# First attention of a four-layer kernel: PSUM banks divided anew between scores and projections, and ScalarE's query copies moved ahead of the exponentials

## The chip, the cores and the metric

The kernel runs on one core of a Trainium2 chip. The metric is the device time of one launch in microseconds. The time before is the median of three runs, 1521.63 us (1520.63 to 1522.21).

## What is computed

Four layers, each an attention and a feed-forward part, over x of 8 x 128 tokens by 256 channels, with a context of the same shape. The change touches the first attention alone. Cut to what matters, it is:

```python
ln_out = _ln(hidden_states, ln_w, ln_b)
q = _ln(_fp8_linear_pertensor(ln_out, wq, wq_scale, q_in_scale).reshape(b, s, g, hpg, d), qln_w, qln_b)
k = _ln(_fp8_linear_pertensor(ln_out, wk, wk_scale, k_in_scale).reshape(b, s, g, d), kln_w, kln_b)
v = _fp8_linear_pertensor(ln_out, wv, wv_scale, v_in_scale).reshape(b, s, g, d)
core = _gqa(q, k, v).reshape(b, s, nh * d)
qx = _ln(_fp8_linear_pertensor(ln_out, wqx, wqx_scale, qx_in_scale).reshape(b, s, g, hpg, d), qxln_w, qxln_b)
kx, vx = jnp.split(jnp.einsum('bsi,oi->bso', cond, w_kv_x), 2, axis=-1)
xout = _gqa(qx, _ln(kx.reshape(b, sc, g, d), kxln_w, kxln_b), vx.reshape(b, sc, g, d)).reshape(b, s, nh * d)
cat = jnp.concatenate([core, xout], axis=-1)
return jnp.einsum('bsi,oi->bso', _div_clamp_fp8(cat, proj_smooth), wproj) * (proj_in_scale * proj_w_scale)
```

`_gqa` is softmax attention with 16 query heads of 128 over 8 key heads. There is a cross part (keys and values from the context) and a core part (from x itself).

## The kernel before

The first attention works on 16 tiles of 128 tokens: the eight tiles of x with the cross part, then the same eight with the core part. Each tile has eight units, one for each step: `UNITS` is k0, q0, k1, q1, v0, q2, v1, q3. A unit is one projection into a PSUM bank of 128 x 512: four heads of queries, of keys or of values. A query or key unit is normalised by head, transposed, and its scores, softmax, mix and output projection follow some steps later.

The order of the work is written by hand. `march` walks over global steps, and at each step every engine issues those functions whose due step it is, in the order of that engine's list. For a unit projected at step s: ScalarE squares it at s; VectorE sums the squares at s+1 (`variance`) and GpSimd makes the reciprocal root (`rstd`); VectorE normalises at s+2 (`normalise`), which reads the projection bank for the last time; TensorE transposes at s+3 (`turn`) and ScalarE copies that out at s+3 (`keep_turned`, L753 for queries, L758 for keys). Query units go on: `score` on TensorE and `row_max` on VectorE at s+4, `exponentials` on ScalarE and `row_inverse` on VectorE at s+5, `scale_probs` on ScalarE at s+6, `turn_probs` on TensorE and `keep_probs` on ScalarE at s+7, `mix` on TensorE and the first half of `round_mixed` on VectorE at s+8, the second half on GpSimd at s+9, `project_out` on TensorE at s+11. Value units are copied out by ScalarE at s+1 (`keep_values`), which frees their bank.

Queries are projected at odd steps, keys and values at even ones. So an even step on TensorE is `turn_probs`, `project_out`, `turn` of a query, and the projection of a key or value unit; an odd step is `score`, `mix`, sometimes `turn` of a key, and the projection of a query unit. Two steps make a period; four periods make a tile. On VectorE an even step is `variance` of a query, `row_inverse`, `normalise` of a key (steps 2 and 4 of a tile only), `add_to_x` (step 2), `quantise` of a part of the next tile's input (three parts a tile, at steps 4, 6 and 8, in the core part; one, at step 4, in the cross part up to its last tiles); an odd step is `variance` of a key (steps 1 and 3), `row_max`, `normalise` of a query, `round_mixed`.

Banks: three rotate over the projections (`bank_of`), one each holds the transposes, the scores, the transposed probabilities, the mix and the output projection. `project` waits until the unit three before it has been read out, `score` waits until the exponentials of the score before have been made (`exp_done`).

Some tiles carry work of their own on ScalarE and VectorE: splitting and centring weights (`prepare` in tile 0, the keys' and values' weights in tile 1, the queries' in tile 4 and at the end of the cross part). The last tile also starts the feed-forward part (`turn_first`, `first_up`) in banks that the attention has left.

Of the kernel before, what the change touches and what calls it, by code (L numbers as in the profile page):

```python
# [186 lines left out]
def layer0_attention(nc, top, res, w, before):  # L187
# [6 lines left out]
    PLAIN = [i for i, unit in enumerate(UNITS) if unit[0] == "v"]  # L194
    QUERY = [i for i, unit in enumerate(UNITS) if unit[0] == "q"]
    NN, NV, NA = len(NORMED), len(PLAIN), len(QUERY)
    BATCH = 4
# [3 lines left out]
    with phase_memory(nc, "l0a") as mem:  # L201
# [98 lines left out]

        proj_bank, turn_bank, score_bank = res.banks[0:3], res.banks[3], res.banks[4]
        probs_bank, mix_bank, out_bank = res.banks[5], res.banks[6], res.banks[7]

        def bank_of(b, i):
            return proj_bank[(b * STEPS + i) % 3]

        at_norm, at_plain, at_query = NORMED, PLAIN, QUERY

        def later(due, n):
            return [s + n for s in due]  # L310
# [5 lines left out]
        F_TURN = [12, 13]  # L316
        f_banks = (bank_of(F_TILE, NORMED[-2]), bank_of(F_TILE, PLAIN[-1]))
        F_UP = [QUERY[-1] + 8, QUERY[-1] + 10, QUERY[-1] + 11, QUERY[-1] + 12]

# [49 lines left out]
        def _(pe):  # L369
# [10 lines left out]
            def project(b, i):  # L380
                kind, u = UNITS[i]
                core = b >= TILES
                G = b * STEPS + i
                if G >= 3:
                    pb, pi = divmod(G - 3, STEPS)
                    if pi in NORMED:
                        norm_done.wait(pe, norm_done.at(pb, NORMED.index(pi) + 1))
                    else:
                        values_done.wait(pe, values_done.at(pb, PLAIN.index(pi) + 1))
# [31 lines left out]
            def score(b, a):  # L421
                turned_out.wait(pe, turned_out.at(b, NORMED.index(QUERY[a]) + 1))
                turned_out.wait(pe, turned_out.at(b, NORMED.index(UNITS.index(("k", a // 2))) + 1))
                exp_done.wait(pe, exp_done.at(b, a))
                for h in range(HU):
                    g = 2 * (a % 2) + h // 2
                    mm = pe.matmul(score_bank[:, h * P:(h + 1) * P], q_t[:, h * P:(h + 1) * P],  # L427
                                   k_t[:, a // 2, g * P:(g + 1) * P], start=True, stop=True)
                mm.then_inc(scored.sem, 1)
# [29 lines left out]
            def turn_first(k):  # L459
                pe.wait_ge(f_rows_ready, 2 * k + 2)  # L460
                if k == 0:
                    norm_done.wait(pe, norm_done.at(F_TILE, NN - 1))
                else:
                    values_done.wait(pe, values_done.at(F_TILE, NV))
                for i in range(2):
                    for c in range(KC):
                        at = (i * KC + c) * P
                        mm = pe.transpose(f_banks[k][:, at:at + P], f_rows[:, 2 * k + i, c * P:(c + 1) * P], res.ident[:])
                mm.then_inc(f_turned, 1)

            def first_up(k):
                if k == 0:
                    norm_done.wait(pe, norm_done.at(VTS - 1, NN))
                    values_done.wait(pe, values_done.at(VTS - 1, NV))
                    turned_out.wait(pe, turned_out.at(VTS - 1, NN))
                    pe.wait_ge(f_xn_ready, 2)
                    pe.wait_ge(res.loaded["l0_e_gate"], 16)
# [14 lines left out]
        def _(v):  # L492
# [115 lines left out]
            def row_max(b, a):  # L608
                scored.wait(v, scored.at(b, a + 1))
                v.tensor_reduce(neg_max[:, a, :], heads(score_bank), X, ALU.max, negate=True).then_inc(max_ready.sem, 1)  # L610

# [63 lines left out]
        def _(act):  # L675
# [70 lines left out]

            def keep_turned(b, n):
                core = b // TILES
                kind, u = UNITS[NORMED[n]]
                turned.wait(act, turned.at(b, n + 1))  # L750
                if kind == "q":
                    scored.wait(act, scored.at(b, u))
                    act.activation(q_t[:], turn_bank[:], ACT.Identity, scale=q_affine[:, core, 0:1],  # L753
                                   bias=q_affine[:, core, 1:2]).then_inc(turned_out.sem, 1)
                else:
                    scored.wait(act, scored.at(b - 1, 2 * u + 2))
                    name = "kln" if core else "kxln"
                    act.activation(k_t[:, u, :], turn_bank[:], ACT.Identity, scale=res.col(f"L0_xattn_{name}_w"),  # L758
                                   bias=res.col(f"L0_xattn_{name}_b")).then_inc(turned_out.sem, 1)

            def exponentials(b, a):
# [4 lines left out]
                for h in range(HU):  # L766
                    done = act.activation(probs[:, a % 2, h * P:(h + 1) * P], score_bank[:, h * P:(h + 1) * P],  # L767
                                          ACT.Exp, bias=neg_max[:, a, h:h + 1], accum_out=row_sum[:, a, h:h + 1])
# [34 lines left out]
            def keep_first(k):  # L803
# [5 lines left out]

            march(VTS, STEPS, [(exponentials, later(at_query, 5)), (scale_probs, later(at_query, 6)),  # L810

                               (keep_values, later(at_plain, 1)), (keep_turned, later(at_norm, 3)),
                               (prepare, range(STEPS)), (keep_probs, later(at_query, 7)), (square, at_norm),
# [2845 lines left out]
```

## Time and profile before

| what | value |
|---|---|
| median of three runs | 1521.63 us |
| the profiled execution's own time | 1520.4 us |
| its span | 1518.6 us |
| mean granted TensorE clock | 0.991 |
| the first attention in it | from about 20 to 470 us |
| PE busy over the span | 1432.2 us (94%) |
| VectorE, ScalarE, GpSimd busy | 887.6, 766.8, 528.6 us |

The engines are PE (TensorE's matmuls), PEld (its weight loads), DVE (VectorE), ACT (ScalarE) and POOL (GpSimd). PE's busy time is that of pipelined instructions whose ends are modelled, and a matmul's duration runs into the next one's. So in this case distances are read from start to start.

### The profile page before, as it was taken

Reading aid. Unit: us, or ns where it says so; the run is one execution under the profiler, and the core shown is the slowest. Engines: PE = TensorE matmul, PEld = TensorE weight load, DVE = VectorE, ACT = ScalarE, POOL = GpSimd, SP = SyncE. Lnnn points to the kernel's source line nnn. Section 1 sums busy time; section 2 is a strip of 40 time slices with the busy share of each in tenths; the row PEclk is TensorE's granted clock in tenths of the full one; section 3 lists DMA queues with packets and bytes.
Section 4 is the critical chain, followed back from the end, with each engine's and each line's share of the span. In section 5 each row is a group of like instructions: output and inputs, shape, how many; then the busy total and the mean of one; then the engine's idle time right before and its main releaser. Section 6 shows DMA issues by size and latency. Waiting matters only on the chain. (4 is left out here: it accounts for less than half of the span.)

```text
span 1518.6 us, 22221 instructions
## 1 busy us (share of the span) xinstructions
PE 1432.2 (94%) x6908; PEld 1030.3 (68%) x6910; DVE 887.6 (58%) x1934; ACT 766.8 (50%) x2122; POOL 528.6 (35%) x519
## 2 busy tenths in 40 slices
PE   3999999899999999999999999998997999999998
PEld 1677777787875555557878888866764666665656
DVE  7788888888875342323454545354677555553322
ACT  4888888888883211110234444444357555554210
POOL 2657577877762000000434243422111333321000
PEclk9999999999999999999999999999998999999999
DMA  5111000200005611112100000000232000011120
GB/s 201 65 58 60 8 5 2 95 1 1 2 1 201 234 51 53 52 49 90 66 1 1 1 1 1 14 15 4 103 148 95 1 1 1 1 29 38 49 67 19
DMA packets 21303, 71.65 MB, mean 47 GB/s; under 512 B 3858, under 2 KB 6290, under 8 KB 18244
## 3 DMA queue, kind: packets, MB, share of 16 engines
q1 hardware_dynamic: 12980, 57.37, 10.1%
q10 hardware_dynamic: 8208, 12.87, 2.7%
q8 instruction: 57, 0.93, 0.2%
q14 instruction: 58, 0.48, 0.1%
HBM read 69.01 MB, written 1.22 MB: 46 GB/s over the span
## 5 line engine op out<-in xcount | busy, mean ns | idle before, releaser
L1190 ACT ACTIVATE l0f_silu<-bank 128x512 f32<-128x512 f32 x48 | 28.6, 597 | 198.3 <-PE bank L1114 188.2
L828 POOL TENSOR_TENSOR l0a_stepped<-l0a_y,l0a_m 128x512 f32<-128x512 bf16 x64 | 74.1, 1158 | 94.4 <-DVE l0a_m L575 92.8
L856 POOL TENSOR_TENSOR l0a_head_rstd<-l0a_head_var,all_minus_half 128x4 f32<-128x4 f32 x96 | 101.8, 1064 | 8.4 <-DVE l0a_head_var L597 8.3
L1293 DVE TENSOR_TENSOR l0f_product<-l0f_silu,bank 128x512 f32<-128x512 f32 x48 | 32.9, 687 | 122.3 <-ACT l0f_silu L1190 122.2
L427 PEld LDWEIGHTS bank<-l0a_k_t,l0a_q_t 128*128 128x128 f32 x512 | 63.9, 193 | 50.1 <-ACT l0a_q_t L753 46.1
L767 ACT ACTIVATE l0a_work<-bank,l0a_neg_max 128x128 f32<-128x128 f32 x256 | 90.2, 370 | 1.2 <-DVE l0a_neg_max L610 1.2
L1722 DVE TENSOR_TENSOR all_weights_a<-bank,all_cols 128x512 f32<-128x512 f32 x64 | 43.9, 690 | 79.7 <-PE bank L1557 47.0
L1126 PEld LDWEIGHTS bank<-all_weights_a,l0f_hidden 128*128 128x128 f32 x384 | 72.9, 190 | 25.2 <-issue 16.7
L427 PE MATMUL bank<-l0a_k_t,l0a_q_t 128*128 128x128 f32 x512 | 72.9, 286 | 17.4 <-ACT l0a_q_t L753 17.1
L1126 PE MATMUL bank<-all_weights_a,l0f_hidden 128*128 128x256 f32 x384 | 88.9, 379 | 0.0
L2315 PE MATMUL bank<-l3a_f_xn_t,all_weights_b 128*128 128x512 f32 x192 | 86.2, 593 | 0.0
L800 ACT ACTIVATE l0a_work<-l0a_work,l0a_row_inv 128x128 f32<-128x128 f32 x256 | 83.1, 425 | 3.7 <-DVE l0a_row_inv L614 3.6
L832 POOL TENSOR_TENSOR l0a_cat<-l0a_stepped,l0a_m 128x512 fp32r<-128x512 f32 x64 | 77.3, 1208 | 10.2 <-issue 9.4
L2611 POOL TENSOR_TENSOR l3a_probs<-l3a_probs,l3a_row_inv 128x512 f32<-128x512 f32 x32 | 33.3, 1042 | 130.0 <-DVE l3a_row_inv L2414 130.0
L1905 ACT ACTIVATE l1a_work<-bank,l1a_exp_bias,l1a_q_scale 128x128 f32<-128x128 f32 x128 | 56.9, 454 | 41.6 <-DVE l1a_exp_bias L1788 41.6
L605 DVE TENSOR_TENSOR l0a_work<-bank,l0a_head_rstd 128x512 f32<-128x512 f32 x96 | 65.1, 678 | 15.6 <-POOL l0a_head_rstd L856 15.5
L739 ACT ACTIVATE l0a_squares<-bank 128x512 f32<-128x512 f32 x96 | 58.3, 608 | 24.7 <-PE bank L409 16.8
L455 PE MATMUL bank<-l0a_wp_high,l0a_cat 128*128 128x256 f32 x256 | 69.5, 304 | 0.1
L597 DVE TENSOR_REDUCE l0a_head_var<-l0a_squares 128x4 f32<-128x516 f32 x96 | 65.6, 683 | 6.2 <-ACT l0a_squares L739 5.0
L418 PE MATMUL bank<-all_ident,l0a_work 128*128 128x128 f32 x384 | 58.9, 276 | 9.7 <-DVE l0a_work L605 9.7
L444 PE MATMUL bank<-l0a_probs_t,l0a_values 128*128 128x256 f32 x256 | 66.0, 380 | 0.2 <-ACT l0a_probs_t L774 0.2
L455 PE MATMUL bank<-l0a_wp_low,l0a_cat 128*128 128x256 f32 x256 | 63.7, 281 | 0.0
(437 smaller groups left out, 3756.6 us busy)
## 6 DMA issues: line engine op xcount, KB each, us to landing
l0f_spread<-l0f_weights ACTq DMA_DIRECT2D x32, 192.0 KB, 2.8
all_weights_a<-in_l_w_q SPq DMA_DIRECT2D x2, 2048.0 KB, 14.2
l0f_spread<-l0f_weights ACTq DMA_DIRECT2D x32, 128.0 KB, 2.8
all_weights_b<-in_l_e_gate_up SPq DMA_DIRECT2D x1, 3200.0 KB, 10.1
all_weights_b<-in_l_e_gate SPq DMA_DIRECT2D x1, 3072.0 KB, 10.1
all_weights_a<-in_l_e_up SPq DMA_DIRECT2D x4, 768.0 KB, 7.1
all_weights_a<-in_l_e_down SPq DMA_DIRECT2D x1, 3072.0 KB, 15.4
l3a_spread<-l3f_weights SPq DMA_DIRECT2D x10, 256.0 KB, 3.4
```

The source lines that it names most:

```text
L427: mm = pe.matmul(score_bank[:, h * P:(h + 1) * P], q_t[:, h * P:(h + 1) * P], k_t[:, a // 2, g * P:(g + 1) * P], start=True, stop=True)
L444: mm = pe.matmul(mix_bank[:, half * 2 * P:(half + 1) * 2 * P], values[:, a // 2, g * P:(g + 1) * P], probs_t[:, half * 2 * P:(half + 1) * ...
L455: mm = pe.matmul(out_bank[:, 0:D], cat[:, a % 2, h * P:(h + 1) * P], part[:, a * HU + h, :], start=(a == 0 and h == 0 and n == 0), stop=(a ...
L597: v.tensor_reduce(head_var[:, m % 2, :], squares[:], X, ALU.add).then_inc(var_ready.sem, 1)
L605: v.tensor_tensor(heads(norm_rows[:, m % 2, :]), heads(bank_of(b, NORMED[n])), along(head_rstd[:, m % 2, :], P), ALU.mult).then_inc(norm_d ...
L767: done = act.activation(probs[:, a % 2, h * P:(h + 1) * P], score_bank[:, h * P:(h + 1) * P], ACT.Exp, bias=neg_max[:, a, h:h + 1], accum_ ...
L800: done = act.activation(pr, pr, ACT.Copy, scale=row_inv[:, a, h:h + 1])
L828: done = g.tensor_tensor(stepped[:, 0:n], value, step, ALU.add)
L832: return g.tensor_tensor(out, stepped[:, 0:n], step, ALU.subtract)
L856: g.tensor_tensor(head_rstd[:, m % 2, :], head_var[:, m % 2, :], res.minus_half[:, 0:HU], ALU.pow)\
L1126: mm = pe.matmul(down_banks[t // 2][:, (t % 2) * D:(t % 2 + 1) * D], hidden[:, n % 2, t * P:(t + 1) * P], w_down[:, j, :], start=(j == 0 a ...
L2315: mm = pe.matmul(bank[:], w_gate_up[:, c, i * (NCH - 1) * P + col:i * (NCH - 1) * P + col + P], f_xn_t[:, c, h * HALF:(h + 1) * HALF], sta ...
```

## The change

Two banks take the projections in turn, and two take the scores; the bank that was the third of the projections is now the first of the scores. `project` waits for the unit two before it, where it waited for the one three before it; `score` waits for the exponentials two before it. On ScalarE `keep_turned` is divided into `keep_queries` and `keep_keys`, and `keep_queries` stands first in the list, ahead of `exponentials`. The two banks of `turn_first` and the wait in front of `first_up` follow the new division.

```diff
+    KEY = [i for i, unit in enumerate(UNITS) if unit[0] == "k"]
...
-        proj_bank, turn_bank, score_bank = res.banks[0:3], res.banks[3], res.banks[4]
+        proj_bank, turn_bank, score_bank = res.banks[0:2], res.banks[3], (res.banks[2], res.banks[4])
...
-            return proj_bank[(b * STEPS + i) % 3]
+            return proj_bank[(b * STEPS + i) % 2]
...
-        f_banks = (bank_of(F_TILE, NORMED[-2]), bank_of(F_TILE, PLAIN[-1]))
+        f_banks = (bank_of(F_TILE, PLAIN[-1]), bank_of(F_TILE, NORMED[-1]))
...
-                if G >= 3:
-                    pb, pi = divmod(G - 3, STEPS)
+                if G >= 2:
+                    pb, pi = divmod(G - 2, STEPS)
...
-                exp_done.wait(pe, exp_done.at(b, a))
+                exp_done.wait(pe, exp_done.at(b, a - 1))
...
-                    mm = pe.matmul(score_bank[:, h * P:(h + 1) * P], q_t[:, h * P:(h + 1) * P],
+                    mm = pe.matmul(score_bank[a % 2][:, h * P:(h + 1) * P], q_t[:, h * P:(h + 1) * P],
...
+                    exp_done.wait(pe, exp_done.at(VTS - 1, NA - 1))
...
-            def keep_turned(b, n):
+            def keep_queries(b, a):
                 core = b // TILES
-                kind, u = UNITS[NORMED[n]]
...
+            def keep_keys(b, u):
+                turned.wait(act, turned.at(b, NORMED.index(KEY[u]) + 1))
...
-            march(VTS, STEPS, [(exponentials, later(at_query, 5)), (scale_probs, later(at_query, 6)),
-
-                               (keep_values, later(at_plain, 1)), (keep_turned, later(at_norm, 3)),
+            march(VTS, STEPS, [(keep_queries, later(at_query, 3)), (exponentials, later(at_query, 5)), (scale_probs, later(at_query, 6)),
+
+                               (keep_values, later(at_plain, 1)), (keep_keys, later(KEY, 3)),
```

Most lines of the changed kernel in the stage stand one or two below their old numbers. On ScalarE, in an even step of the cross part and the odd step behind it (`l0a_q_t` is the queries' copy, `l0a_work` the exponentials and then the scaling, `l0a_probs_t` the copy of the transposed probabilities), before:

```order
L767 ACTIVATE l0a_work,l0a_row_sum<-bank4,l0a_neg_max 128x128 x4
L753 ACTIVATE l0a_q_t<-bank3,l0a_q_affine 128x512
L774 ACTIVATE l0a_probs_t<-bank5 128x512
L739 ACTIVATE l0a_squares<-bank1 128x4x128
L800 ACTIVATE l0a_work<-l0a_work,l0a_row_inv 128x128 x4
L758 ACTIVATE l0a_k_t<-bank3,all_cols 128x512
```

and now:

```order
L753 ACTIVATE l0a_q_t<-bank3,l0a_q_affine 128x512
L769 ACTIVATE l0a_work,l0a_row_sum<-bank2,l0a_neg_max 128x128 x4
L776 ACTIVATE l0a_probs_t<-bank5 128x512
L741 ACTIVATE l0a_squares<-bank0 128x4x128
L802 ACTIVATE l0a_work<-l0a_work,l0a_row_inv 128x128 x4
L760 ACTIVATE l0a_k_t<-bank3,all_cols 128x512
```

The copy of the queries, which waits for the transposes at the end of TensorE's even step, has moved in front of the four exponentials; nothing else has moved.

On TensorE the instructions stand as they did; what has changed is the banks, and with them what the waits are for. From a value unit's projection to the next query's, in the core part, before:

```order
L409 MATMUL bank2<-l0a_wv_high,l0a_xq 128x512 [waits l0a_w_low,l0a_quant_done,l0a_norm_done]
L409 MATMUL bank2<-l0a_wv_low,l0a_xq 128x512
L427 MATMUL bank4<-l0a_k_t,l0a_q_t 128x128 [waits l0a_exp_done,l0a_turned_out]
L427 MATMUL bank4<-l0a_k_t,l0a_q_t 128x128 x3
L444 MATMUL bank6<-l0a_probs_t,l0a_values 128x256 [waits l0a_mixed_read,l0a_values_done,l0a_probs_t_ready]
L418 MATMUL bank3<-all_ident,l0a_work 128x128 [waits l0a_turned_out,l0a_norm_done]
L409 MATMUL bank0<-l0a_wq_high,l0a_xq 128x512 [waits l0a_w_low,l0a_quant_done,l0a_norm_done]
```

and now:

```order
L410 MATMUL bank0<-l0a_wv_high,l0a_xq 128x512 [waits l0a_w_low,l0a_quant_done,l0a_norm_done]
L410 MATMUL bank0<-l0a_wv_low,l0a_xq 128x512
L428 MATMUL bank2<-l0a_k_t,l0a_q_t 128x128 [waits l0a_exp_done,l0a_turned_out]
L428 MATMUL bank2<-l0a_k_t,l0a_q_t 128x128 x3
L445 MATMUL bank6<-l0a_probs_t,l0a_values 128x256 [waits l0a_mixed_read,l0a_values_done,l0a_probs_t_ready]
L419 MATMUL bank3<-all_ident,l0a_work 128x128 [waits l0a_turned_out,l0a_norm_done]
L410 MATMUL bank1<-l0a_wq_high,l0a_xq 128x512 [waits l0a_w_low,l0a_quant_done,l0a_norm_done]
```

Keys and values now always use bank 0 and queries always bank 1, so the value unit here waits for the normalisation of the key unit two steps before it, and the query for that of the query before it.

On VectorE the order is the same; in an even step with a key's normalisation and the odd step behind it, it now reads:

```order
L616 RECIPROCAL l0a_row_inv<-l0a_row_sum 128x4 [waits l0a_exp_done]
L607 TENSOR_TENSOR l0a_work<-bank0,l0a_head_rstd 128x512 [waits l0a_turned,l0a_rstd_ready]
L571 TENSOR_SCALAR l0a_yq16<-l0a_yq16 128x256 [waits l0a_quant_scaled]
L573 TENSOR_SCALAR l0a_e16<-l0a_yq16 128x256
L577 TENSOR_SCALAR l0a_mq16<-l0a_e16 128x256
L612 TENSOR_REDUCE l0a_neg_max<-bank2 128x4 [waits l0a_scored]
L607 TENSOR_TENSOR l0a_work<-bank1,l0a_head_rstd 128x512 [waits l0a_turned,l0a_rstd_ready]
```

Bank 0 is read out for the last time by the second row and bank 1 by the last; each stands behind a row that waits for another engine.

## Rows read from the trace of the kernel before

**Rows 1.** The page, busy time by engine, and one of its groups of instructions.
```profile
PE 1432.2 (94%) x6908; PEld 1030.3 (68%) x6910; DVE 887.6 (58%) x1934; ACT 766.8 (50%) x2122; POOL 528.6 (35%) x519
...
L597 DVE TENSOR_REDUCE l0a_head_var<-l0a_squares 128x4 f32<-128x516 f32 x96 | 65.6, 683 | 6.2 <-ACT l0a_squares L739 5.0
```
**Rows 2.** Stretches of cross and core: length, busy PE, PEld, DVE, ACT, POOL, clock, DMA.
```profile
140.00:180.00 40.00, 39.34 (x234) 30.99 (x233) 35.05 (x72) 33.28 (x107) 25.98 (x26) 1.00 0.02 5
340.00:380.00 40.00, 37.07 (x237) 31.39 (x236) 34.32 (x76) 35.42 (x117) 31.26 (x33) 1.00 0.01 1
```
**Rows 3.** PE's waits over the span: us in total, times, longest.
```profile
PE bank L427 <- ACT l0a_q_t L753: 17.1, 30, 1.3
```
**Rows 4.** Timeline of one period of the core part: start, duration, engine, instruction.
```profile
352.17 0.35 ACT L767 ACTIVATE l0a_work<-bank,l0a_neg_max 128x128 f32<-128x128 f32 x1
...
352.28 0.60 PE L418 MATMUL bank<-all_ident,l0a_work 128*128 128x128 f32 x4
...
352.64 0.48 PE L409 MATMUL bank<-l0a_wk_high,l0a_xq 128*128 128x512 f32 x1
...
353.54 0.79 ACT L753 ACTIVATE l0a_q_t<-bank,l0a_q_affine 128x512 f32<-128x512 f32 x1
353.69 0.18 DVE L614 RECIPROCAL l0a_row_inv<-l0a_row_sum 128x4 f32<-128x4 f32 x1 [0.18 <-ACT l0a_work L767]
353.79 0.67 DVE L605 TENSOR_TENSOR l0a_work<-bank,l0a_head_rstd 128x512 f32<-128x512 f32 x1
354.20 0.62 ACT L774 ACTIVATE l0a_probs_t<-bank 128x512 f32<-128x512 f32 x1
...
354.38 1.16 PE L427 MATMUL bank<-l0a_k_t,l0a_q_t 128*128 128x128 f32 x8 [0.58 <-ACT l0a_q_t L753]
...
354.68 0.63 ACT L739 ACTIVATE l0a_squares<-bank 128x512 f32<-128x512 f32 x1
...
355.38 1.03 PE L444 MATMUL bank<-l0a_probs_t,l0a_values 128*128 128x256 f32 x4
...
356.24 0.60 PE L418 MATMUL bank<-all_ident,l0a_work 128*128 128x128 f32 x4
356.38 0.68 DVE L610 TENSOR_REDUCE l0a_neg_max<-bank 128x4 f32<-128x512 f32 x1
...
356.60 0.48 PE L409 MATMUL bank<-l0a_wq_high,l0a_xq 128*128 128x512 f32 x1
...
356.97 0.68 DVE L605 TENSOR_TENSOR l0a_work<-bank,l0a_head_rstd 128x512 f32<-128x512 f32 x1
...
359.00 0.60 PE L418 MATMUL bank<-all_ident,l0a_work 128*128 128x128 f32 x4
```
**Rows 5.** Timeline, the first and the last operation of one `quantise` on VectorE.
```profile
361.29 0.83 DVE L569 TENSOR_SCALAR l0a_yq<-l0a_yq 128x256 bf16<-128x256 bf16 x1
...
362.49 0.23 DVE L575 TENSOR_SCALAR l0a_mq<-l0a_e 128x256 bf16<-128x256 bf16 x1
```
**Rows 6.** Timeline: one cross projection, and VectorE's `add_to_x`, once a tile.
```profile
106.13 1.88 PE L399 MATMUL bank<-l0a_wkx,l0a_ctx_t 128*128 128x512 f32 x4
...
88.17 0.47 DVE L627 SCALAR_TENSOR_TENSOR all_x<-bank,l0a_out_scale,all_x 128x256 f32<-128x256 f32 x1
...
220.77 0.48 DVE L627 SCALAR_TENSOR_TENSOR all_x<-bank,l0a_out_scale,all_x 128x256 f32<-128x256 f32 x1
...
304.15 0.47 DVE L627 SCALAR_TENSOR_TENSOR all_x<-bank,l0a_out_scale,all_x 128x256 f32<-128x256 f32 x1
...
431.63 0.47 DVE L627 SCALAR_TENSOR_TENSOR all_x<-bank,l0a_out_scale,all_x 128x256 f32<-128x256 f32 x1
```
**Rows 7.** Start of the stage: one stretch of a microsecond (columns of Rows 2), then PE's timeline.
```profile
38.00:39.00 1.00, 0.61 (x3) 0.61 (x4) 1.00 (x2) 0.71 (x2) 1.00 (x2) 0.50 0.00 0
...
38.39 1.12 PE L418 MATMUL bank<-all_ident,l0a_work 128*128 128x128 f32 x4 [3.29 <-DVE l0a_work L605]
...
42.71 1.71 PE L427 MATMUL bank<-l0a_k_t,l0a_q_t 128*128 128x128 f32 x8
44.26 0.60 PE L418 MATMUL bank<-all_ident,l0a_work 128*128 128x128 f32 x4
```

More of the change, by code:

```diff
@@ L461, in turn_first @@
                 if k == 0:
-                    norm_done.wait(pe, norm_done.at(F_TILE, NN - 1))
+                    values_done.wait(pe, values_done.at(F_TILE, NV))
                 else:
-                    values_done.wait(pe, values_done.at(F_TILE, NV))
+                    norm_done.wait(pe, norm_done.at(F_TILE, NN))
                 for i in range(2):
@@ L609, in row_max @@
                 scored.wait(v, scored.at(b, a + 1))
-                v.tensor_reduce(neg_max[:, a, :], heads(score_bank), X, ALU.max, negate=True).then_inc(max_ready.sem, 1)
+                v.tensor_reduce(neg_max[:, a, :], heads(score_bank[a % 2]), X, ALU.max, negate=True).then_inc(max_ready.sem, 1)
             def row_inverse(b, a):
@@ L745, in keep_values @@
                 act.activation(values[:, n, :], bank_of(b, PLAIN[n])[:], ACT.Copy).then_inc(values_done.sem, 1)
-            def keep_turned(b, n):
+            def keep_queries(b, a):
                 core = b // TILES
-                kind, u = UNITS[NORMED[n]]
[L750 to L759, printed above, removed]
+                turned.wait(act, turned.at(b, NORMED.index(QUERY[a]) + 1))
+                scored.wait(act, scored.at(b, a))
+                act.activation(q_t[:], turn_bank[:], ACT.Identity, scale=q_affine[:, core, 0:1],
+                               bias=q_affine[:, core, 1:2]).then_inc(turned_out.sem, 1)
+            def keep_keys(b, u):
+                turned.wait(act, turned.at(b, NORMED.index(KEY[u]) + 1))
+                scored.wait(act, scored.at(b - 1, 2 * u + 2))
+                name = "kln" if b >= TILES else "kxln"
+                act.activation(k_t[:, u, :], turn_bank[:], ACT.Identity, scale=res.col(f"L0_xattn_{name}_w"),
+                               bias=res.col(f"L0_xattn_{name}_b")).then_inc(turned_out.sem, 1)
             def exponentials(b, a):
@@ L766, in exponentials @@
                 for h in range(HU):
-                    done = act.activation(probs[:, a % 2, h * P:(h + 1) * P], score_bank[:, h * P:(h + 1) * P],
+                    done = act.activation(probs[:, a % 2, h * P:(h + 1) * P], score_bank[a % 2][:, h * P:(h + 1) * P],
                                           ACT.Exp, bias=neg_max[:, a, h:h + 1], accum_out=row_sum[:, a, h:h + 1])
```

## The prediction

> **What bounds the kernel now.** I read the page's busy times first. TensorE is busy for 94% of the span [rows 1], so the reader should look for what TensorE waits for, and for what a change could put in front of it. The stretches by stage come next. In the cross part TensorE is busy for 39.34 us of 40, in the core part for 37.07; ScalarE and VectorE are at 83 to 89% in both [rows 2]. All three engines are near full, so slack on any of them is small. The list of waits then names what the change aims at: scores that wait for the copied queries, 17.1 us in 30 waits [rows 3]. Last, the timeline of one period shows why [rows 4]. ScalarE starts its exponentials at 352.17, before TensorE has begun to turn the next queries (352.28), and copies them only behind the exponentials, at 353.54. The score starts at 354.38, 0.58 us late.
>
> The same rows show what the early exponentials serve. They release VectorE's reciprocal (353.69), behind which stands the normalisation of a key unit (353.79). That frees a projection bank, and with three banks nobody needs it soon: the next key or value projection in that bank is a whole unit away.
>
> **The clock of one period.** Let 0 be the start of the turning of queries (352.28). From start to start [rows 4]: turn to projection 0.36; the transposes end at 0.60. A projection of four matmuls gives way to the next work after about 1.0 (estimate: the 2.40 from 356.60 to 359.00 hold one, with the turned probabilities and the output projection). Score to mix 1.00, mix to the key's turn 0.86, that to the query projection 0.36, and from there to the next turn 2.40. On ScalarE the copy of queries takes 0.66 to the next instruction, and a score may start 0.84 after the copy's start; the four exponentials take 1.37. On VectorE the reciprocal starts 1.52 after the first exponential, the normalisation 0.10 later; it lasts 0.67, and I give TensorE 0.05 to see it, as it needed after the copy. `row_max` to the next start is 0.59.
>
> **What is removed.** The score no longer waits for the exponentials, and the copy of queries no longer stands behind them. At most the 17.1 us of [rows 3] can be won. The exp_done wait itself was never last: the wait that ended last is the copy. So the second score bank is worth nothing beyond letting the copy go first.
>
> **What is added, keys and values.** Key unit 1 now waits for the normalisation of key unit 0, and value unit 0 for that of key unit 1: both belong to the same even step. The chain is closed: turn ends 0.60, the copy starts 0.64, the exponentials 1.30, the reciprocal 2.82, the normalisation 2.92, done at 3.59, and the projection starts at 3.64, where it started at 0.36. Behind it on TensorE stand the score, the mix and everything else; nothing covers the 3.04 us. This holds in two periods of four (call them A). The other two (B) wait for value unit copies of the step before, which are long done.
>
> **What is added, queries.** A query projection now waits for the normalisation of the query before, which stands behind `row_max` of the score of the same step. The least distance from score to query projection is then 1.16 + 0.05 + 0.59 + 0.67 + 0.05, about 2.5. TensorE has 1.86 of other work for that time, or 2.22 with a key's turn.
>
> **The mix.** It needs the copied probabilities, which stand behind copy and exponentials on ScalarE: 2.67 + 0.62 + 0.05 = 3.34 at the earliest.
>
> **The sum by period, core part** (measured: 127.5 us for five tiles, 25.5 a tile [rows 6]).
> - A at step 4: projection 3.64, score 4.64, its end 5.80, `row_max` 5.85, normalisation 6.44, query projection 7.16, next turn 9.56.
> - A at step 2: the key's variance comes in between. Its projection ends near 4.8, its square takes 0.6, the variance 0.68 [rows 1, 4]: 0.3 more, 9.86.
> - B at step 6: score 1.48, mix 3.34 to 4.20. VectorE: reciprocal 2.82, `quantise` 1.43 [rows 5] to 4.35, `row_max`, normalisation 4.94, query projection 5.66, next turn 8.06.
> - B at step 0: a variance more, 8.7.
> Together 36.2, 10.7 more a tile; eight tiles, 86 us.
>
> **Cross part** (132.6 us for five tiles, 26.5 a tile [rows 6]). A projection from the context lasts 1.88 against 1.16, 0.72 more [rows 4, 6]: A gives 10.3 and 10.6. B has no `quantise`: at step 6 the score starts 2.1, ends 3.3, and the next turn is at 7.0; at step 0 it is 8.2, since square and variance of the key come first. Together 36.1, 9.6 more; eight tiles, 77 us.
>
> **Tiles with weight work.** Centring and splitting stand on VectorE between its reciprocal and its `row_max`, so what was slack now delays query projections; the first and the last tile, on the other hand, have fewer full periods. I put the two at +7 together, with bounds of -15 and +40.
>
> So 86 + 77 + 7 = 170 us at full clock.
>
> **The clock.** At the start of the stage TensorE stood still for 3.29 us waiting for a normalisation; work went on at 38.39 with a granted clock of 0.50, and a score took 1.71 instead of 1.16; at 44.26 a turn is back at 0.60 [rows 4, 7]. 0.50 is the lower level, 1.2 GHz of 2.4. The new gap in A is 3.04 us, near to that row. The lower bound is nothing; the upper is 5.9 us at half speed, 3 us lost for each of the 32 gaps, 94 us. I take 1.6 each, since part of the work in it is overtaken by VectorE's chain and not each gap need drop the clock: 50 us.
>
> The Trainium skill ("TensorE: Matmul & The Clock Gate", HAM oscillation) describes a loop in which TensorE waits each round and its clock falls each round. By that rule all 32 gaps would pay, and the sum would be 264 and not 220. The row at 38.39 agrees with it for one gap; no row shows a repeated one.
>
> The skill ("Perfetto Trace Analysis", Matmuls) also asks that independent groups rotate through different banks so that reading one out overlaps the next one's matmuls. By that rule alone two and two is as good a rotation as three and one and the 17 us would be won; the timeline weighs against it, as a projection's read-out ends two steps later [rows 4].
>
> **Nothing** I count for: the wait in front of `first_up` (the last exponentials come steps earlier), the other banks of `turn_first` (their last readers are two or more steps old), SP and GpSimd (nothing moves there; they wait along).
>
> **Sum.** 1520.4 of the profiled execution + 170 + 50 = 1740; the median stands 1.2 above it: 1742.
>
> **Rivals.**
> 1. The clock stays high through gaps of 3.04 us. For: 3.29 is longer, and ScalarE's chain may be a little shorter than I have it. Against: it fell there. 1692. Chance 0.22.
> 2. Only the keys' wait and the mix bind, the query chain on VectorE is hidden. A then takes 9.3 and B 6.6 in the core part, 10.0 and 6.6 in the cross part: 32 and 33 a tile, +6.3 and +6.7, about 104, so 1626. Against: `row_max` cannot start before the score. Chance 0.08.
> 3. The clock also falls in B's gaps (0.7 and 1.5 us close together) and stays down longer: 3 us an A, 1.5 a B, 9 a tile, 144: 1836. Chance 0.15.
> 4. Faster: the projection banks are free in time. That would need a key's normalisation done within 0.36 of the turn's start, so VectorE would have to run it before the reciprocal that waits for the exponentials. Then the 17.1 us go: 1504. The order on VectorE speaks against it. Chance 0.02.
> 5. Gain and new waits cancel to within 0.2%: 0.01.
> The forecast has 0.52.
>
> 0.2% (3 us) is about what a measurement can tell from no change. Faster 0.02, same 0.01, slower 0.97. The range: between rivals 2 and 3, with the bounds of weight work, 1635 to 1850.
>
> **What would show it.** In the profile after: TensorE waiting for VectorE's normalisation at the projection line, about 3 us each, 32 times, about 90 to 100 us, and again 0.3 to 1.5 us before each query projection; the wait for the copied queries gone; ScalarE idle before the copy; a turn-to-turn distance near 9.7, 9.7, 8, 8.5; tiles 36 us apart at full clock; granted clock below 1 in the stage. The argument is wrong if key and value projections start within a microsecond of the turn, or if tiles stay below 30 us.

## The result and the profile after

The changed kernel takes 1745.36 us (median of four runs, 1742.6 to 1750.92) against 1521.13 us. The ratio is 1.148, with a 95% interval of 1.146 to 1.150. The forecast was 1742, its range 1635 to 1850. The profiled execution took 1743.94 us, of which 1742.2 are the span. From the page of the changed kernel, the busy times by engine and the clock in 40 slices:

```profile
PE 1518.2 (87%) x6910; PEld 1085.4 (62%) x6910; DVE 862.8 (50%) x1934; ACT 775.7 (45%) x2122; POOL 520.6 (30%) x519
...
PEclk9988978889988889999999999999989999999999
```

TensorE goes from 94% of the span [rows 1] to 87%, and the clock shows eights and a seven in ten of the slices 3 to 15 (87 to 653 us), the attention's. (TensorE's busy time has grown by 86 us although its work is the same: part of that is the slower clock.) The other engines' busy times moved by no more than 3%, over a longer span.

Where the time went is told first by the marks of `add_to_x`, one for each tile, as in [rows 6]. Timeline of the changed kernel, VectorE:

```profile
108.72 0.48 DVE L629 SCALAR_TENSOR_TENSOR all_x<-bank,l0a_out_scale,all_x 128x256 f32<-128x256 f32 x1
...
329.79 0.47 DVE L629 SCALAR_TENSOR_TENSOR all_x<-bank,l0a_out_scale,all_x 128x256 f32<-128x256 f32 x1
...
447.11 0.47 DVE L629 SCALAR_TENSOR_TENSOR all_x<-bank,l0a_out_scale,all_x 128x256 f32<-128x256 f32 x1
...
641.14 0.48 DVE L629 SCALAR_TENSOR_TENSOR all_x<-bank,l0a_out_scale,all_x 128x256 f32<-128x256 f32 x1
...
692.94 0.48 DVE L629 SCALAR_TENSOR_TENSOR all_x<-bank,l0a_out_scale,all_x 128x256 f32<-128x256 f32 x1 [4.82 <-PE bank L456]
```

Five cross tiles take 221.1 us (108.72 to 329.79), 44.2 each, where it was 26.5. Five core tiles take 194.0, 38.8 each, where it was 25.5. The last mark stands at 692.94 and stood at 470.69: 222.3 us later. The span grew by 223.6, so the loss lies in the first attention, but for about 1 us.

The list of TensorE's waits over the span then says what it waits for:

```profile
PE bank L410 <- DVE l0a_work L607: 101.2, 53, 3.6
PE bank L400 <- DVE l0a_work L607: 50.3, 16, 5.1
PE bank L445 <- ACT l0a_probs_t L776: 13.5, 19, 0.7
...
PE bank L428 <- ACT l0a_q_t L753: 1.7, 2, 0.9
```

L410 and L400 are the projections (L400 those from the context). They wait 151.5 us for VectorE's normalisations; in the kernel before no such wait stands in the list. The mix waits 13.5 us for the copied probabilities. The score's wait for the copied queries, 17.1 us in [rows 3], has fallen to 1.7. So the change took away the wait that it aimed at, and put about ten times as much waiting in its place.

One period, to be laid beside [rows 4]; a period of the core part in the changed kernel, TensorE, then ScalarE, then VectorE:

```profile
480.42 0.60 PE L419 MATMUL bank<-all_ident,l0a_work 128*128 128x128 f32 x4
484.09 0.79 PE L410 MATMUL bank<-l0a_wk_high,l0a_xq 128*128 128x512 f32 x1 [3.07 <-DVE l0a_work L607]
...
485.96 1.91 PE L428 MATMUL bank<-l0a_k_t,l0a_q_t 128*128 128x128 f32 x8
...
490.05 0.49 PE L410 MATMUL bank<-l0a_wq_high,l0a_xq 128*128 128x512 f32 x1
...
492.47 0.60 PE L419 MATMUL bank<-all_ident,l0a_work 128*128 128x128 f32 x4
...
481.05 0.78 ACT L753 ACTIVATE l0a_q_t<-bank,l0a_q_affine 128x512 f32<-128x512 f32 x1 [1.29 <-PE bank L419]
481.73 0.36 ACT L769 ACTIVATE l0a_work<-bank,l0a_neg_max 128x128 f32<-128x128 f32 x1
...
483.26 0.18 DVE L616 RECIPROCAL l0a_row_inv<-l0a_row_sum 128x4 f32<-128x4 f32 x1 [3.36 <-ACT l0a_work L769]
483.36 0.68 DVE L607 TENSOR_TENSOR l0a_work<-bank,l0a_head_rstd 128x512 f32<-128x512 f32 x1
```

With the turn of the queries at 480.42 as 0, the copy starts at 0.63, the exponentials at 1.31, the reciprocal at 2.84, the key's normalisation at 2.94 and the key projection at 3.67. The forecast chain had 0.64, 1.30, 2.82, 2.92 and 3.64. VectorE waited 3.36 us for the exponentials and TensorE 3.07 us for VectorE: neither was busy, and each was held by the instruction at the head of its own queue. The whole period takes 12.05 us, the slow clock behind the gap included.

The clock, in two stretches of the core part, one behind such a gap and one without (columns as in Rows 2):

```profile
484.00:490.00 6.00, 5.91 (x19) 5.06 (x20) 3.41 (x8) 1.76 (x5) 1.01 (x1) 0.50 0.00 1
...
503.00:511.00 8.00, 6.55 (x42) 5.21 (x41) 4.58 (x12) 5.59 (x18) 5.01 (x6) 1.00 0.01 3
```

Behind the gap TensorE worked for six microseconds at half its clock: the score at 485.96 lasts 1.91, against 1.16 in [rows 4]. In the period from 503.33, whose two waits are 0.7 us each (the mix at 506.69, the query projection at 508.54), the clock stays at 1.00.

### The profile page after: what moved, and what is told of

It reads as the page before. It is cut to its first block and busy times, and to the rows that moved or that the text cites. A ratio compares the mean times of both kernels' runs of the same rounds, so it can differ in the third digit from the quotient of the medians.

```text
span 1742.2 us, 22223 instructions
## 1 busy us (share of the span) xinstructions
PE 1518.2 (87%) x6910; PEld 1085.4 (62%) x6910; DVE 862.8 (50%) x1934; ACT 775.7 (45%) x2122; POOL 520.6 (30%) x519
## 5 line engine op out<-in xcount | busy, mean ns | idle before, releaser
L858 POOL TENSOR_TENSOR l0a_head_rstd<-l0a_head_var,all_minus_half 128x4 f32<-128x4 f32 x96 | 97.3, 1014 | 96.5 <-DVE l0a_head_var L599 96.4
L410 PE MATMUL bank<-l0a_wq_high,l0a_xq 128*128 128x512 f32 x128 | 61.2, 478 | 53.8 <-DVE l0a_work L607 52.0
L428 PEld LDWEIGHTS bank<-l0a_k_t,l0a_q_t 128*128 128x128 f32 x512 | 82.9, 234 | 30.4 <-issue 19.5
L616 DVE RECIPROCAL l0a_row_inv<-l0a_row_sum 128x4 f32<-128x4 f32 x64 | 11.4, 178 | 176.0 <-ACT l0a_work L769 176.0
L445 PE MATMUL bank<-l0a_probs_t,l0a_values 128*128 128x256 f32 x256 | 79.6, 440 | 14.8 <-ACT l0a_probs_t L776 13.5
L428 PE MATMUL bank<-l0a_k_t,l0a_q_t 128*128 128x128 f32 x512 | 85.4, 321 | 1.7 <-ACT l0a_q_t L753 1.7
L753 ACT ACTIVATE l0a_q_t<-bank,l0a_q_affine 128x512 f32<-128x512 f32 x64 | 49.8, 777 | 62.7 <-PE bank L419 62.7
L456 PE MATMUL bank<-l0a_wp_high,l0a_cat 128*128 128x256 f32 x256 | 75.4, 324 | 0.0
L410 PEld LDWEIGHTS bank<-l0a_wq_high,l0a_xq 128*128 128x128 f32 x128 | 26.0, 203 | 74.8 <-DVE l0a_work L607 68.5
```

Source lines behind the costliest of these rows:

```text
L410: mm = pe.matmul(bank[:], xq[:, b % 2, WHICH[kind], c, :], part[:, c, u * BANK:(u + 1) * BANK], start=(c == 0 and n == 0), stop=(c == KC - ...
L428: mm = pe.matmul(score_bank[a % 2][:, h * P:(h + 1) * P], q_t[:, h * P:(h + 1) * P], k_t[:, a // 2, g * P:(g + 1) * P], start=True, stop=True)
L445: mm = pe.matmul(mix_bank[:, half * 2 * P:(half + 1) * 2 * P], values[:, a // 2, g * P:(g + 1) * P], probs_t[:, half * 2 * P:(half + 1) * ...
L456: mm = pe.matmul(out_bank[:, 0:D], cat[:, a % 2, h * P:(h + 1) * P], part[:, a * HU + h, :], start=(a == 0 and h == 0 and n == 0), stop=(a ...
L858: g.tensor_tensor(head_rstd[:, m % 2, :], head_var[:, m % 2, :], res.minus_half[:, 0:HU], ALU.pow)\
```

## The experiments

Twelve kernels were run. The kernel before, run beside them, took 1520.42 to 1520.84 us; against that the change costs 225 us. Below, 0.63 or 3.67 "of the period" count from the start of the queries' turn. Diffs are against the changed kernel where nothing else is said; `...` stands for lines left out. The two parts of the change come first.

### The order on ScalarE alone

```diff
-        proj_bank, turn_bank, score_bank = res.banks[0:2], res.banks[3], (res.banks[2], res.banks[4])
+        proj_bank, turn_bank, score_bank = res.banks[0:3], res.banks[3], (res.banks[4], res.banks[4])
...
-            return proj_bank[(b * STEPS + i) % 2]
+            return proj_bank[(b * STEPS + i) % 3]
...
-                if G >= 2:
-                    pb, pi = divmod(G - 2, STEPS)
+                if G >= 3:
+                    pb, pi = divmod(G - 3, STEPS)
...
-                exp_done.wait(pe, exp_done.at(b, a - 1))
+                exp_done.wait(pe, exp_done.at(b, a))
```

> The changed order on ScalarE alone: three projection banks and one score bank as before, the copy of queries ahead of the exponentials. My theory (most of the loss is the third projection bank, the order adds to it): the score now waits for exponentials that start at 1.30 of the period and so starts at 2.83, the mix at 3.83, the next turn at 7.45 or 7.1, against 25.5 to 26.5 a tile 29.1: 50 us slower than before, 1571 (1545 to 1600). Rival, the order is the whole cause and the banks cost nothing: about 1745. Rival, the order costs nothing by itself: 1521.

Measured: 1570.26 us (1568.37 to 1571.1), ratio 1.0326 (1.0311 to 1.0341), 50 us slower than before. Its waits:

```profile
PE bank L428 <- ACT l0a_work L769: 68.9, 62, 2.4
```

That is the score waiting for the exponentials, which now stand behind the copy, 62 times in 64 scores. Five core tiles take 29.3 us each; 29.1 was worked out. The order costs 50 us where there is one score bank, and the mean clock is 0.990 (0.991 before).

### The banks alone

```diff
-            march(VTS, STEPS, [(keep_queries, later(at_query, 3)), (exponentials, later(at_query, 5)), (scale_probs, later(at_query, 6)),
+            march(VTS, STEPS, [(exponentials, later(at_query, 5)), (scale_probs, later(at_query, 6)),
...
-                               (keep_values, later(at_plain, 1)), (keep_keys, later(KEY, 3)),
+                               (keep_values, later(at_plain, 1)), (keep_queries, later(at_query, 3)), (keep_keys, later(KEY, 3)),
```

> The banks alone: two for projections and two for scores as in the changed kernel, ScalarE in its old order. My theory: the key's normalisation is done at 2.2 of the period and not at 3.6, so key and value projections start at 2.2; periods 8.2, 8.5, 7.0, 7.3 in the core part, 0.7 more in two of four in the cross part: 31 and 32.4 a tile, about 95 us more than before plus some 15 for the clock, 1630 (1600 to 1670). PE's wait at key and value projections about 1.5 us each. Rival, order alone is the cause: 1521. Rival, banks alone are the cause: 1745.

Measured: 1608.52 us (1608.21 to 1612.65), ratio 1.0588 (1.0568 to 1.0607), 88 us slower than before; 21 less than worked out, but inside what the theory gave, and far from both rivals. The mean clock is 0.988, so the 15 us that I had put in for it did not come. Its waits:

```profile
PE bank L410 <- DVE l0a_work L607: 63.0, 63, 2.6
PE bank L400 <- DVE l0a_work L607: 29.4, 16, 5.1
```

The 16 waits at L400, cross projections of keys and values, are 1.8 us on average, against 3.1 in the changed kernel. So 50 and 88 make 138, and the change as a whole costs 225: 87 more. The order puts the exponentials behind the turn, and the banks put the projection behind the exponentials. Only together do they close a chain from one TensorE instruction to the next one in its queue.

The chain by itself is the smaller part of these 87, as far as the core part shows it. In the changed kernel three periods in a row run at full clock; they take 9.91, 9.57 and 7.62 us:

```profile
443.57:470.67 27.10, 19.02 (x118) 15.62 (x117) 14.97 (x37) 17.77 (x54) 13.51 (x15) 1.00 0.00 1
```

The fourth takes 8.23 at full clock (from 551.70), so a tile is 35.3, or 9.8 more than before. A core tile costs 3.8 more with the order alone and 5.0 more with the banks alone (30.5), 8.9 together, both at a clock of 1.00 there. So the chain adds about 1 us a tile to the two. The other 3.5, up to the measured 38.8, are the clock, which neither part brings down there.

### The third bank back

The kernel has eight PSUM banks (`res.banks`), and three for projections, two for scores and one for each of the four other uses are nine. The mix can go into that score bank which is idle in its step:

```diff
-        proj_bank, turn_bank, score_bank = res.banks[0:2], res.banks[3], (res.banks[2], res.banks[4])
-        probs_bank, mix_bank, out_bank = res.banks[5], res.banks[6], res.banks[7]
+        proj_bank, turn_bank, score_bank = res.banks[0:3], res.banks[3], (res.banks[4], res.banks[6])
+        probs_bank, out_bank = res.banks[5], res.banks[7]
+
+        def mix_bank(a):
+            return score_bank[(a + 1) % 2]
...
+                mixed_read.wait(pe, mixed_read.at(b, a - 2))
...
+                exp_done.wait(pe, min(exp_done.at(b, a + 2), VTS * NA))
```

> The changed kernel with its third projection bank back. The room comes from the mix, which is written into that one of the two score banks that is idle in its step. Theory: with the read-out of three units back is free, all waits at the projection lines go, the clock is back at 1.00 in the stage, and what stays is the mix that waits for the copied probabilities until 3.34: periods 7.0 and 6.6, 27.1 a tile, 1540 (1525 to 1560). Rival, that the order on ScalarE is the cause: still over 1700.

Measured: 1548.54 us (1548.39 to 1549.06), ratio 1.0186 (1.017 to 1.0201), mean clock 0.991. With the third bank back, 197 of the 225 us are gone. The wait at the projections is gone from the list, and what stays is the mix:

```profile
PE bank L450 <- ACT l0a_probs_t L781: 25.8, 38, 0.7
```

28 us remain, nine more than expected; the core tile is at 27.5, where 27.1 was worked out, and the cross tile at 28.4.

### Two score banks with the old order

The same kernel with the two lines of ScalarE's list as in "The banks alone".

> Three projection banks, two score banks (shared with the mix as in the run with the third bank back) and ScalarE's old order. It is the control for the shared banks, and it asks whether a second score bank gives anything by itself. Theory: the score waits for the copied queries, not for the exponentials, so nothing is gained and nothing lost: 1521, within 3 us, with the waits of rows 3 unchanged near 17 us. Rival, a second score bank is worth what the waits show: 1504.

Measured: 1520.25 us (1518.25 to 1523.24), ratio 1.0000 (0.9991 to 1.0010). The score's wait is the old one, 16.3 us in 27 waits. So sharing the mix's bank costs nothing, and a second score bank by itself gives nothing: the wait for the exponentials was never the last one.

### Who reads the bank last, and where it stands in its queue

The next two keep the changed kernel's banks and move VectorE's instructions. First the keys' normalisation alone, ahead of the reciprocal (`normalise_keys` and `normalise_queries` are `normalise` for the one kind and the other):

```diff
-            march(VTS, STEPS, [(variance, later(at_norm, 1)), (row_inverse, later(at_query, 5)),
-                               (row_max, later(at_query, 4)), (normalise, later(at_norm, 2)),
+            march(VTS, STEPS, [(variance, later(at_norm, 1)), (normalise_keys, later(KEY, 2)), (row_inverse, later(at_query, 5)),
+                               (row_max, later(at_query, 4)), (normalise_queries, later(at_query, 2)),
```

> The changed kernel with the keys' normalisation alone moved ahead of row_inverse; the queries' stays behind row_max. It parts the two new waits. Theory: the 3 us waits before key and value projections go, those before query projections stay at 0.5 to 2 us each; periods about 7.6, 8.5, 7.7, 8.2 in the core part, and 1 to 2 us less in the cross part, clock nearly full: 1625 (1590 to 1660). Rival, the queries' wait is hidden behind the mix: 1545. Rival, the wait only moves over to the queries: over 1700.

Measured: 1642.49 us (1641.61 to 1643.84), ratio 1.0803 (1.0788 to 1.0818), inside what the theory gave: 103 us of 225 are gone. The mean clock is 0.980 and was 0.945, so a part of the 103 is the clock. Then all normalisations first:

```diff
-            march(VTS, STEPS, [(variance, later(at_norm, 1)), (row_inverse, later(at_query, 5)),
-                               (row_max, later(at_query, 4)), (normalise, later(at_norm, 2)),
+            march(VTS, STEPS, [(normalise, later(at_norm, 2)), (variance, later(at_norm, 1)), (row_inverse, later(at_query, 5)),
+                               (row_max, later(at_query, 4)),
```

> The changed kernel with VectorE's normalisations first in its list, ahead of variance, row_inverse and row_max. Theory: what hurts with two banks is that the last reader of a bank stands behind instructions that wait for this step's exponentials and score. With it first, waits at the projection lines fall from 151.5 us to under 30, the mix at 3.34 stays: 27 a tile, 1545 (1525 to 1580). Rival, two banks are too few wherever the reader stands: over 1650.

Measured: 1589.67 us (1586.92 to 1593.15), ratio 1.0456 (1.044 to 1.0472), mean clock 0.983: 53 more. The waits at the projections, with the keys first and with all first:

```profile
PE bank L410 <- DVE l0a_work L607: 76.0, 75, 3.6
...
PE bank L400 <- DVE l0a_work L607: 9.8, 14, 4.2
```

```profile
PE bank L410 <- DVE l0a_work L607: 34.9, 36, 2.7
...
PE bank L400 <- DVE l0a_work L607: 10.6, 14, 3.6
```

From 151.5 us the waits fall to 85.8 and then to 45.5. I had forecast under 30 and 1545: the mechanism is borne out, the remainder mis-sized. At 1590 two banks are still 41 us behind the kernel with three and the same order on ScalarE (1548.54). Three banks with the normalisations first were not run, so what moving them costs or gives by itself stays open. In one place of this run VectorE's own queue is in the way: at 382.47 a key's normalisation starts as soon as the last step of `round_mixed` is through, and the value projection follows at 383.21, 0.49 us late.

### How much of it is the clock

```diff
+            def idle_work(b, a):
+                if a > 1:
+                    return
+                mixed_read.wait(pe, mixed_read.at(b, a + 1))
+                for n in range(22):
+                    pe.matmul(mix_bank[:, 0:P], res.ident[:], res.ident[:], start=True, stop=True)
...
-                               (turn, later(at_norm, 3)), (project, range(STEPS))])
+                               (turn, later(at_norm, 3)), (idle_work, later(at_query, 9)), (project, range(STEPS))])
```

> The changed kernel with 22 extra matmuls (identity by identity, 128 columns, into the idle mix bank; nothing reads them) in each of the 32 places where TensorE waits for a key's normalisation. It sizes the clock's share. Theory: the waits stay as long, since the matmuls end before the wait does, but the granted clock in the stage goes from 0.87 to above 0.95, and the time falls by 40 to 70 us to 1690 (1675 to 1710). Rival, the clock costs nothing because VectorE's chain hides the slow matmuls: 1745 or a little above.

Measured: 1751.57 us (1749.03 to 1753.38), ratio 1.1518 (1.150 to 1.1535), far from the 1690 expected, and it looks like the rival. But the timeline shows that the added work did not fit into the gap:

```profile
493.44 5.08 PE L465 MATMUL bank<-all_ident 128*128 128x128 f32 x44
498.27 0.48 PE L410 MATMUL bank<-l0a_wv_high,l0a_xq 128*128 128x512 f32 x1
```

The 22 calls became 44 instructions, and the projection came 5.3 us behind the turn at 493.00 and not 3.67. So it was run again with `range(12)`.

> The changed kernel with 12 extra matmuls in each of the 32 gaps and not 22. In the run with 22 each call became two instructions, 44 of them took 5.08 us, and the projection started 5.3 us behind the turn where the wait alone ends at 3.67: 1.6 us too long, 32 times 51 us. If the clock's share is near 45 us the two cancel, as that run's 1752 has it, and 12 calls (2.8 us, inside the gap) give 1700 (1690 to 1712) with the same clock of about 0.97. If the clock costs nothing: 1745. If the 22 had cost nothing by their length: 1752.

Measured: 1702.44 us (1701.98 to 1705.98), ratio 1.1200 (1.1185 to 1.1216). More work in TensorE's queue makes the kernel 43 us faster. Here the added matmuls end inside the gap; of the wait 0.39 us is left, and it still ends with the normalisation:

```profile
489.30 0.60 PE L419 MATMUL bank<-all_ident,l0a_work 128*128 128x128 f32 x4
489.73 2.84 PE L465 MATMUL bank<-all_ident 128*128 128x128 f32 x24
492.97 0.50 PE L410 MATMUL bank<-l0a_wk_high,l0a_xq 128*128 128x512 f32 x1 [0.39 <-DVE l0a_work L614]
...
499.20 0.60 PE L419 MATMUL bank<-all_ident,l0a_work 128*128 128x128 f32 x4
```

The projection stands at 3.67 of the period, as in the changed kernel, and the period is 9.90 where that of the changed kernel was 12.05. The stretch from 60 to 660 us of the changed kernel, then of this one:

```profile
60.00:660.00 600.00, 448.94 (x2213) 349.32 (x2214) 307.53 (x683) 341.94 (x1033) 271.68 (x273) 0.87 0.04 15
```

```profile
60.00:660.00 600.00, 520.37 (x3159) 425.50 (x3158) 324.71 (x727) 364.11 (x1103) 289.57 (x288) 0.96 0.05 17
```

The granted clock goes from 0.87 to 0.96, and 43 us with it, as was expected (1700). As 0.96 is not 1.00, 43 is a lower bound of the clock's share. At most 182 of the 225 us are the waits and what stands behind them. In two of the five core tiles of this run the clock is 1.00, and they take 35.3 us, as the changed kernel's own periods gave it:

```profile
420.65:455.95 35.30, 30.55 (x200) 25.93 (x200) 19.79 (x50) 23.23 (x72) 19.15 (x20) 1.00 0.01 1
```

### Looking for a faster kernel

With three projection banks and two score banks, the copy of queries can stand between the second and third of the four exponentials. ScalarE then fills the time before the turn's end with two of them. Against the kernel with the third bank back (`exp_head` and `exp_tail` are the first and the last two exponentials):

```diff
-            march(VTS, STEPS, [(keep_queries, later(at_query, 3)), (exponentials, later(at_query, 5)), (scale_probs, later(at_query, 6)),
+            march(VTS, STEPS, [(exp_head, later(at_query, 5)), (keep_queries, later(at_query, 3)), (exp_tail, later(at_query, 5)), (scale_probs, later(at_query, 6)),
```

> Three projection banks, two score banks shared with the mix, and the copy of queries between the second and the third of the four exponentials, so that ScalarE fills the time before the turn's end with two of them. Theory: the copy starts at 0.64 of the period, the score at 1.48 where it was 2.10, the mix at 2.7 where it was 3.10: up to 0.4 us a period in the core part, less in the cross part, where TensorE is full: 1510 (1503 to 1519), faster than before. Rival, ScalarE is the bound and nothing is won: 1521. Rival, the later reciprocal takes it back: over 1525.

Measured: 1520.83 us (1519.3 to 1523.65), ratio 1.0007 (0.9998 to 1.0016): no difference, where 1510 was expected. The score's wait is gone, 1.7 us in 2 waits from 60 to 460 us where it was 16.5 in 28. In the same stretch the turns wait more:

```profile
PE bank L422 <- DVE l0a_work L612: 8.6, 16, 1.6
```

Before, it was 3.8 us in 8. Four core tiles pass in 25.05 us each and not 25.3, and that is lost again elsewhere (cross tiles 26.6 and not 26.5). TensorE's named waits are some 9 us fewer and the time is the same, so they come back in places that the list does not name; where, was not followed through. One case is seen in the timeline: the projection at 346.98 starts 0.82 behind its turn and not 0.36, just after GpSimd has written the input that it reads. So it isn't shown what bounds this kernel.

```profile
346.21 0.67 POOL L846 TENSOR_TENSOR l0a_xq<-l0a_stepped,l0a_mq 128x256 fp32r<-128x256 f32 x1
```

Since the normalisations in turn waited for GpSimd's reciprocal root, I put the root ahead of GpSimd's rounding passes: in this kernel, in the one with all normalisations first, and in the kernel before. The edit is the same in all three:

```diff
-            march(VTS, STEPS, [(round_mixed, later(at_query, 9)), in_tile(F_ROWS_TILE, first_rstd, F_ROWS[0:1]), (rstd, later(at_norm, 1)),
+            march(VTS, STEPS, [(rstd, later(at_norm, 1)), (round_mixed, later(at_query, 9)), in_tile(F_ROWS_TILE, first_rstd, F_ROWS[0:1]),
```

> The kernel with the copy between the exponentials, and GpSimd's reciprocal root ahead of its two rounding passes in an even step. In the run without it the score's wait was gone, but turns waited for the normalisation (15.9 us in 19 waits), which waited for the reciprocal root on GpSimd (10.2 us in the core part). Theory: with the root first these waits go and the gain shows, 1510 (1503 to 1517). Rival, TensorE's own work is the bound by now: 1520. Rival, the rounding comes too late for the output projection: over 1525.

> The changed kernel with normalisations first on VectorE (1590) and the reciprocal root first on GpSimd as well. Theory: of the 45.5 us that TensorE still waited at the projection lines, most is the root that stands behind the rounding passes; with it first 1560 (1548 to 1575), the rest being the mix that waits and the normalisation behind `round_mixed`. Rival, it is VectorE's own queue alone: 1590.

> The kernel before with the reciprocal root first on GpSimd and nothing else: the control for the run with the copy between. Theory: there TensorE waits for the copied queries and not for normalisations (2.7 us in the core part), so 1518 to 1521. Rival, the root alone brings what that run brings: 1510.

Measured, in this order: 1544.21 us (1542.49 to 1545.04), ratio 1.0153 (1.0139 to 1.0167); 1614.14 us (1613.24 to 1614.42), ratio 1.0613 (1.0597 to 1.063); 1530.67 us (1528.38 to 1531.97), ratio 1.0065 (1.0053 to 1.0078). All three expectations failed, and in each case the edit costs: 23, 24 and 10 us. For the first, the rival that the rounding comes too late has the right size and the right wait. From its waits, from 60 to 460 us, TensorE, then GpSimd:

```profile
PE bank L461 <- POOL l0a_cat L846: 18.6, 31, 1.5
```

```profile
POOL l0a_head_rstd L870 <- DVE l0a_head_var L604: 93.4, 53, 4.4
```

The root waits 93.4 us for VectorE's variance (1.6 without the edit) and holds up the rounding behind it, and the output projection, whose wait was in no list before, waits 18.6 us. In the third it waits 11.3. It is the fault of the change once more, on another engine: an instruction whose input comes late, moved ahead of one whose input was ready. In the second, GpSimd's root waits 158.5 us for the variance (46.8 without the edit). VectorE's waits for the root fall from 11.8 to 1.4 us, and yet TensorE's at the projections rise from 45.5 to 67.2; by which instruction is not shown. No kernel was found that is faster than the one before.

## Why the prediction was right, and where its parts were off

- **The chain to key and value projections** was right to 0.03 us in its first period (3.67 for 3.64), and the wait of 3.07 us at the projection is there. That it is the order and the banks together was shown by taking each away and by moving the keys' normalisation.
- **"At most the 17.1 us can be won"** held, and the true gain is nearer to nothing: the wait fell by 15.4 us, but in the kernel with the copy between, where it is gone too, the time did not fall (1520.83). The second score bank gave nothing by itself (1520.25).
- **The mix at 3.34** is there: up to 0.73 us late in the periods without a key's normalisation, 13.5 us in all.
- **The core part at full clock** was sized well: 35.3 us a tile for 36.2. The period at step 2 is 9.91 (forecast 9.86), that at step 4 9.57 (9.56). The period at step 6 is 7.62 for 8.06: `quantise` takes 0.84 there and not the 1.43 of [rows 5]. The period at step 0 is 8.23 for 8.7.
- **The clock** was a term of 50 and measured at least 43. In the five core tiles it fell after eight of the ten gaps of 3.07 us, so the sum of 264, by which every gap pays, was too much. It also fell in three places with shorter gaps, which the sum of 220 did not have. At full clock the five tiles would take 176.6 and they took 194.0: 17 us for eleven falls, 1.6 each, which is the term of the sum. Rival 1 (the clock stays) and rival 3 (9 us a tile, where it is 3.5) are refuted by that.
- **The tiles with weight work** were the term that was mis-sized. I gave them 7 us together with the first and the last tile. With the idle work in the gaps, cross tiles take 40.9 us each where 36.1 were worked out, about 24 us in the five tiles shown; some of that is still the clock, which is 0.94 over them. One of the five is at 1.00 and takes 38.0. All five carry such work: by the kernel's lists (`KV_LOW`, `Q_CENTRE`, `EARLY_QUANT`) it does not end in tiles 1 and 4 but runs on to tile 7, and I overlooked the early input parts that start in tile 3. One such place: in the changed kernel a splitting pass of 1.20 us at 177.31 and three passes of input quantisation after it put `row_max` at 179.34, and the query projection at 180.68 waits 1.83 us. Centring, from 216.94 to 219.86, makes the one at 221.12 wait 2.63, and the longest wait of a query projection is 3.58. The forecast had 0.3 to 1.5.
- **The other way**, I counted eight full tiles in each part. But the first two tiles together lost 21 us, the three tiles at the seam 34, and the stretch after the last full tile 13: 67, where six tiles of the sum, clock included, make 80. The five cross tiles lost 88 where it had 64. The errors nearly cancel, and that 1742 stands beside 1745 is in part luck.

Rival 2, that the query chain is hidden, is refuted by the waits of the query projections in the changed kernel (0.72 us at 508.54, 1.83 at 180.68) and by the run with the keys first: 76.0 us of waits in 75 query and core projections were left there.

## What to carry to other kernels

Ask of a PSUM bank not how many there are but which instruction reads it last, what stands ahead of that one in its queue, and whether any of that waits for the engine that is to have the bank. Here two projection banks cost 197 us more than three where the last reader stood behind instructions of the same step, 88 where those ran early, and 41 where the reader ran ahead of them. Moving an instruction to the front of an in-order queue takes from everything behind it the time that it waits; here the exponentials, which had filled the wait for free, became the wait.

Where gaps of about 3 us recur on TensorE, price the clock with the gap (here 3.5 of the 13.3 us that a core tile lost), and test it by filling the gap with work that nobody reads.

## What was not expected of the hardware

VectorE's first pass of `quantise`, 128 x 256 in bf16, took 0.83 us in [rows 5] and takes 0.23 in the changed kernel. In the kernel before GpSimd was in a rounding pass of its own from 360.87 for 1.16 us, and the stretched pass (361.29 to 362.12) ends 0.09 us after it:

```profile
360.87 1.16 POOL L832 TENSOR_TENSOR l0a_cat<-l0a_stepped,l0a_m 128x512 fp32r<-128x512 f32 x1 [0.16 <-issue]
```

```profile
496.18 0.23 DVE L571 TENSOR_SCALAR l0a_yq<-l0a_yq 128x256 bf16<-128x256 bf16 x1
```

In the changed kernel GpSimd stood idle at that time, until 497.18. The timelines hold 93 passes of this size in each kernel. In the kernel before 37 of them take longer than 0.35 us; each of the 37 begins while GpSimd is in a rounding pass, and ends 0.07 to 0.09 us after such a pass does. Another 18 begin in a rounding pass too, at its very start or in its last 0.3 us, and are not stretched, and neither are the 28 that begin during GpSimd's reciprocal root. By which rule the two engines hinder each other is not shown. In the changed kernel 92 of the 93 meet an idle GpSimd, and none is stretched. So the slower kernel has the faster passes, and a duration read from the one trace (1.43 us for `quantise`) was too long for the other (0.84).
